# A recurrent kernel on one core: where GpSimd takes the difference of state and candidate

## The reference

```
# GRU, for every step t
z  = sigmoid(xz + hz);  r = sigmoid(xr + hr)
hc = tanh(xh + r * hh)
hn = z * h + (1 - z) * hc            # = hc + z * (h - hc)
# attention score of the state
emb = [h, news - h, news, h * news]
a = relu(emb @ W1 + b1);  a = relu(a @ W2 + b2);  at = sigmoid(a @ W3 + b3)
# second recurrence over the states
u = sigmoid(xu + g @ Uu);  r = sigmoid(xr + g @ Ur);  c = tanh(xc + r * (g @ Uc))
g = (1 - at * u) * g + (at * u) * c
# head: batch norm of [g_final, news], three dense layers
```

## Time and profile before

| | |
|---|---|
| median of 3 runs | 1980.85 us (1979.35 to 1981.06) |
| the profiled execution | 1982.23 us, its span 1980.4 us |
| TensorE busy | 1937.3 us, 98% of the span |
| GpSimd busy | 1642.1 us, 83% |
| VectorE busy | 1499.0 us, 76% |
| ScalarE busy | 1452.0 us, 73% |
| mean busy share of the 16 DMA engines | about 0.15 in the steady part |

### The profile page before, as it was taken

How to read it: one execution, slowest core, us unless ns; L and a number is a source line. 1 busy time by engine, 2 the same in 40 slices (tenths; PEclk the granted TensorE clock), 3 DMA queues, 4 the chain that set the end, 5 groups by cost and what they waited for, 6 DMA issues and landing times.

```text
span 1980.4 us, 29691 instructions
## 1 busy us (share of the span) xinstructions
PE 1937.3 (98%) x9180; PEld 860.6 (43%) x9180; DVE 1499.0 (76%) x2356; ACT 1452.0 (73%) x2464; POOL 1642.1 (83%) x1396
## 2 busy tenths in 40 slices
PE   6799999999999999999999999999999999999998
PEld 2244444444444444444444444444444444444443
DVE  6677777777777777777777777777777777777775
ACT  5577777777777777777777777777777777777764
POOL 5688888888888888888888888888888888888862
PEclk9899999999999999999999999999999999999999
DMA  3111111111111111111111111111211111111110
GB/s 105 48 54 49 70 50 51 48 69 48 50 70 50 48 64 53 52 49 69 48 48 69 53 48 51 66 48 53 69 48 48 69 48 53 48 69 48 38 44 22
DMA packets 37146, 108.15 MB, mean 55 GB/s; under 512 B 4282, under 2 KB 4538, under 8 KB 30594
## 3 DMA queue, kind: packets, MB, share of 16 engines
q1 hardware_dynamic: 37122, 107.86, 15.4%
HBM read 107.43 MB, written 0.42 MB: 54 GB/s over the span
## 4 chain that ended last, share of the span: by engine, by line
PE 92%; POOL 3%; DVE 2%; issue 1%; ACT 1%; DMA 1%; SPq 0%; DVEq 0%; POOLq 0%; ACTq 0%
PE ps L762 29%; PE ps L763 29%; PE ps L764 29%; PE ps L825 3%; PE ps L816 1%; POOL hn_lo L282 1%; POOL h_lo L288 1%; POOL d L331 1%; DMA score<-score_rows 0%; POOL gus L321 0%; ACT hn_hi L372 0%; DMA x<-in_xs 0%; POOL g_lo L312 0%; POOL x_lo L335 0%; DVE ps L570 0%
## 5 line engine op out<-in xcount | busy, mean ns | idle before, releaser
L762 PE MATMUL ps<-h_hi,w_hi 128*128 128x512 f16 x1384 | 526.5, 380 | 16.2 <-DVE a_lo L650 5.9
L763 PE MATMUL ps<-h_lo,w_hi 128*128 128x512 f16 x1384 | 525.7, 380 | 0.0
L764 PE MATMUL ps<-h_hi,w_lo 128*128 128x512 f16 x1384 | 525.4, 380 | 0.0
L282 POOL TENSOR_TENSOR hn_lo<-hn,hn_hi 128x512 f16<-128x512 f32 x200 | 232.9, 1164 | 187.1 <-ACT hn_hi L372 187.1
L276 POOL TENSOR_TENSOR hn<-h,news 128x512 f32<-128x512 f32 x200 | 256.0, 1280 | 86.5 <-DVE h L668 78.6
L446 ACT ACTIVATE ps<-gt,p_rest 128x512 f32<-128x512 f32 x196 | 135.3, 690 | 216.8 <-DVE gt L665 216.8
L321 POOL TENSOR_TENSOR gus<-gu,score 128x512 f32<-128x512 f32 x200 | 254.8, 1274 | 5.4 <-DMA score<-score_rows 3.8
L331 POOL TENSOR_TENSOR d<-h,hc 128x512 f32<-128x512 f32 x196 | 249.9, 1275 | 6.0 <-ACT hc L474 6.0
L762 PE MATMUL ps<-x_hi,w_hi 128*128 128x512 f16 x599 | 229.3, 383 | 14.4 <-POOL x_lo L335 5.1
L312 POOL TENSOR_TENSOR g_lo<-g,g_hi 128x512 f16<-128x512 f32 x196 | 228.1, 1164 | 17.6 <-ACT g_hi L478 17.6
L656 DVE TENSOR_TENSOR gt<-gr,ps 128x512 f32<-128x512 f32 x196 | 134.9, 688 | 140.3 <-ACT gr L481 140.3
(11 more groups left out here) (123 smaller groups left out, 3706.1 us busy)
## 6 DMA issues: line engine op xcount, KB each, us to landing
x<-in_xs SPq DMA_DIRECT2D x200, 256.0 KB, 3.1
score<-score_rows SPq DMA_DIRECT2D x50, 1024.0 KB, 4.7
news<-in_xs SPq DMA_DIRECT2D x1, 1024.0 KB, 8.5
score_rows<-s_rows SPq DMA_DIRECT2D x50, 8.0 KB
p_rest<-in_pack_rest SPq DMA_DIRECT2D x1, 776.0 KB, 9.3
p_att<-in_pack_att SPq DMA_DIRECT2D x1, 322.0 KB, 6.4
p_gru<-in_pack_gru SPq DMA_DIRECT2D x1, 195.0 KB, 2.6
p_state<-in_pack_state SPq DMA_DIRECT2D x1, 192.0 KB, 8.5
```

The costliest lines, as they stand in the source:

```text
L282: g.tensor_tensor(hn_lo[:, k, :], hn[:, k, :], hn_hi[:, k, :], ALU.subtract).then_inc(hnlo_ready, 1)
L762: m.matmul(ps[:, bank, :], w_hi[:, w, :], hi, start=start, stop=False)
L763: m.matmul(ps[:, bank, :], w_hi[:, w, :], lo, start=False, stop=False)
L764: return m.matmul(ps[:, bank, :], w_lo[:, w, :], hi, start=False, stop=stop)
```

## The change

In GpSimd's `slot`, the block that waits for `hc_ready` and takes the difference `d` moves from behind `state_news_low` and `state_low` to ahead of them, and so right behind `gus`. It applies to all slots, in the loop and outside. The waits, operands and sizes stay as they are.

```
--- before.py
+++ after.py
@@ -319,16 +319,16 @@
                     pool.wait_ge(gu_ready, at(LAG + 1))
                     pool.wait_ge(score_landed, landed(LAG + 1))
                     g.tensor_tensor(gus[:, k, :], gu[:, k, :], score[:, c, :], ALU.mult).then_inc(gus_ready, 1)
+                if has(low) and low >= NC:
+                    c, k = low % NC, low % 2
+                    pool.wait_ge(hc_ready, at(0))
+                    g.tensor_tensor(d[:, k, :], h32[:, c, :], hc[:, k, :], ALU.subtract).then_inc(d_ready, 1)
                 if AHEAD <= low < NC:
                     state_low(low, low + 1)
                     state_news_low(low, low + 1)
                 if has(low - 1) and low - 1 >= NC:
                     state_news_low(low - 1, at(1))
                     state_low(low - 1, at(1))
-                if has(low) and low >= NC:
-                    c, k = low % NC, low % 2
-                    pool.wait_ge(hc_ready, at(0))
-                    g.tensor_tensor(d[:, k, :], h32[:, c, :], hc[:, k, :], ALU.subtract).then_inc(d_ready, 1)
                 if has(low + 1) and low + 1 >= NC:
                     c = (low + 1) % NC
                     pool.wait_ge(xhi_ready, at(-1))
```

More of the change, by code:

```diff
@@ L327, in slot @@
                     state_low(low - 1, at(1))
[L328 to L331, removed]
                 if has(low + 1) and low + 1 >= NC:
```

## The result

| | before | changed |
|---|---|---|
| median | 1980.95 us (1979.35 to 1981.3) | 2163.85 us (2162.78 to 2164.85) |
| profiled execution, its span | 1982.23, 1980.4 | 2162.78, 2160.7 |
| four slots in the steady part | 38.20 us | 41.79 us |

The ratio is 1.0924, interval 1.0908 to 1.0939: the change costs 183 us. The forecast was 2159, with 2143 to 2175 for the forecast itself and 2117 to 2190 with the rivals (a) and (d).

A forecast was written before the change was run, and what follows sets the result against it. TensorE's stream was taken to bound the steady state. Steady part 163.3, start 14 and end 1.4 sum to 178.7 on the profiled 1982.23, so 2160.9; the median is 1.4 lower, predicted 2159 us, range 2143 to 2175.

The forecast's parts named there:

- (a): Rival: gus comes in time, so only the loop through TensorE binds; 2117 to 2126 us, chance 0.12.
- (d): Rival: an unseen hand-over or wait costs 0.1 us more in each round; +18, up to 2190 us, chance 0.08.
- Step one and two: From TensorE's slot start to d, then over hn_lo and h_lo to its next start: 6.36+3.64 = 10.00 us against 9.07.
- Step three: GpSimd's own loop from one d to the next, over gus, t and hc: 10.38 us.
- D: The start of d on GpSimd, put at 6.36 us after TensorE's slot start, 6.32 after a long slot.
- Step four: Both loops together in the steady part: 41.74 us for four slots against 38.21, +163.3 us in all.
- the long slot: Every fourth TensorE slot, with the scores and `attention_2` as well: 11.02 us where others last 9.07.
- Step five: The start, ten intervals from the first d to item 14's: 103 us against 89, +14.
- my high end: The start's upper case: a weak clock slows twelve matmuls by 2.5 us per slot in four more slots, +24 in all.
- Step six: The end: after the last d TensorE's next slot starts 3.64 instead of 2.26 us later, +1.4.
- (b): Rival: not slower, h_lo arrives in time, which needs hc 0.93 us earlier; 1972 to 1981 us, chance 0.03.
- (c): Rival: new stalls make TensorE's clock fall; four slots about 51.4, some 2590 us, chance 0.03.

The follow-up runs named there:

- late_mult: The changed kernel with VectorE's multiply by gus moved behind the addition that completes t; 2122.27 us, ratio 1.0708.
- x_ahead_changed: The changed kernel with x_lo moved ahead of d (order x_lo, d, hn_lo, h_lo); 2121.02 us, ratio 1.0707.
- gus_first: The changed kernel with gus moved ahead of hn in GpSimd's order; 2197.03 us, ratio 1.1085.
- start_only: The kernel before with the changed order in slots 4 to 15 alone; 1999.85 us, ratio 1.0096.
- wait_only: The kernel before with only the wait for hc added ahead of hn_lo, d staying behind h_lo; 2172.87 us, ratio 1.0964.
- wait_late_mult: The kernel before with the wait for hc ahead of hn_lo and VectorE's multiply by gus behind the addition that completes t; 2083.65 us, ratio 1.0513.
- x_ahead_wait: The kernel before with the wait for hc ahead of hn_lo and x_lo ahead of that wait; 2150.31 us, ratio 1.0853.
- x_wait_late_mult: x_ahead_wait with VectorE's multiply by gus behind the addition that completes t; 2038.61 us, ratio 1.0288.

## Why the prediction was right

**Step one and two, the loop through TensorE (10.00).** The hand-over from GpSimd to TensorE is 0.14 in the changed kernel as in rows 8 (1109.24 to 1109.38). The loop itself is covered there by the longer round; it shows bare at the start (intervals of 9.98, 9.99 and 9.99 us) and in late_mult (9.97, in some slots 9.89). TensorE's waits for h_lo show as 0.74, 1.18 and 1.18 us where 0.9, 1.3 and 1.3 were named, because the bracket counts from the end of a matmul that lasts 0.38 us, 0.16 more than the distance to the next.

**Step three, GpSimd's round (10.38).** Measured 10.40 and 10.41. The hand-over to VectorE, which I had put at 0.06 between 0.03 and 0.14, is 1114.02-1113.92 = 0.10; the two others are 0.04 and 0.07, for 0.03 and 0.08, and from D to the end of gus it is 8.18 for 8.20. Together that is the difference of 0.02. late_mult and x_ahead_changed each open this round at another place and end together; gus_first lengthens it.

**Step four, the mix (41.74).** Measured 41.79: three rounds of 10.40 and the rest, 10.58, where the long slot comes in. The steady stretch is 2077.4-144.48 = 1932.92 us against 1766.85, **+166.1 for +163.3**.

**Step five, the start (+14).** The ten intervals are 104.16 us against 88.84, **+15.3**. (The first d came 1.9 us earlier in this execution, at 40.3. The new order has no part in that: start_only, with the same order in this stretch, has it at 42.4.) As a sum the step is right, in its parts only half. The late intervals are 9.98 to 10.8, as said. The early ones are 11.49, 11.0, 12.05 and 11.21, longer than I took for the middle value. From d to TensorE's next start it is 3.63 or 3.64 us, as in the sum; the excess is between TensorE's start and the next d, 7.4 to 8.4 us for 6.3 (62.69 to 70.06, 73.69 to 82.11). TensorE waits 1.7, 4.2, 4.2 and 3.9 us for h_lo in these slots, the granted clock of two stretches around the waits of 4.2 is 0.79 and 0.57 (part of each at the 1.2 GHz level), and the first matmuls after them take 0.59 and 0.58 us instead of 0.38. So part of it is the clock, as in my high end, but not all: the first of the four has the clock at 1.00 and d 7.85 behind TensorE's start. The first interval is shorter than before, 7.25 for 8.35, but the next is longer by nearly as much (11.49 for 10.47), so that I was right to count nothing for an early d. Two stretches of the start (columns as in rows 2), and the matmuls that waited:

```profile
60.00:64.00 4.00, 1.31 (x4) 0.52 (x5) 3.54 (x5) 0.63 (x1) 4.00 (x5) 0.79 0.00 0
72.00:76.00 4.00, 2.31 (x6) 0.87 (x7) 3.86 (x6) 0.63 (x1) 3.87 (x4) 0.57 0.04 16
```

```profile
62.69 0.59 PE L762 MATMUL ps<-h_hi,w_hi 128*128 128x512 f16 x1 [4.21 <-POOL h_lo L288]
...
73.69 0.58 PE L762 MATMUL ps<-h_hi,w_hi 128*128 128x512 f16 x1 [4.18 <-POOL h_lo L288]
```

start_only puts the start at +19.0 in the median, so 14 was somewhat low; 2.6 us of it lie in slots 14 and 15, which are in the steady term of my sum.

**Step six, the end (+1.4).** From the last d to the end of the span 83.3 us, before 82.5: +0.8.

**The sum.** 166.1+15.3+0.8 = 182.2, for 178.7; the earlier first d leaves 180.3 between the two profiled executions. The medians moved by 182.9.

**The rivals.** (a), that gus comes in time, is refuted by the wait of 0.39 us for gus and by late_mult: a kernel in which hc doesn't need gus takes 40.9 us for four slots, about what (a) gives (41.0), and the changed one 41.8. (b), not slower, failed where it was said to: hc ends at 1116.07, A+6.69. (c), that the clock falls in the steady part, is refuted by the row from 400 to 1000 us: waits of 0.74 to 1.18 us at the start of three slots in four, and granted clock 1.00. The Trainium skill (TensorE: Matmul & The Clock Gate, "A second HAM failure mode: psum-queue depth-cycling") says of another kernel that micro-idles between groups of matmuls made the clock oscillate. The steady part of this trace doesn't agree; at the start, with its longer waits, the clock does fall, in the kernel before as well (0.80). (d) had the right sign and a quarter of the size: 0.02 to 0.03 a round for 0.1.

**Where the method failed.** It was in the experiments. wait_only, wait_late_mult and x_ahead_wait are 27, 64 and 135 us above the upper ends of their expectations, each by a loop that I had not listed: over d and ScalarE's list behind the long slot (and by a longer start); over x_lo; over d, the state and gus, and again over ScalarE's list. In the prediction I had checked the deadlines of h_lo, hn and gus, and for the changed order those are the ones that bind; for the new orders I took over that list, and it was no longer complete. gus_first and x_wait_late_mult met their expectations partly by luck, as said there.

## What to carry to other kernels

A wait that is moved forward holds up everything behind it on its engine, so the cost of a new order is the longest closed path through all engines, summed from start-to-start distances, and not the delay of one consumer; an engine with 17% idle time can become the bound without one instruction more. For each new order list the deadline of every instruction behind the wait afresh, since the three large misses here were loops left off the list. In an ordered queue with several producers, put what is ready into the time ahead of the wait: one instruction ahead of d instead of none (h_lo, d, hn_lo) took the cost from 9.2% to 0.3%. A loop can also bind in one slot of four alone, where another engine's list is longer there; compare the slots one by one and not only their mean.

## What the runs showed of the hardware that was not expected

- With waits of 0.7 to 1.2 us in three of four slots of some 10.4 us, TensorE kept the full granted clock of 1.00 for the whole steady part. At the start it fell to 0.57 in single stretches of 4 us, behind waits of about 4.2 us in slots of 11 to 12 us. The kernel before shows 0.59 as well, from 56 to 60 us, with a wait of 2.5 us in that stretch.
- The time from the end of one engine's instruction to the start of another's that waited for it differs between places and is steady at each: GpSimd to TensorE 0.14 us for h_lo but 0.05 for x_lo (1134.42 to 1134.47 in wait_only), GpSimd to VectorE 0.10 for gus but 0.03 for d (1112.64 to 1112.67 in x_ahead_wait), ScalarE to GpSimd 0.07, VectorE to ScalarE 0.04. In the round over gus they make 0.21 of 10.40 us.
